# Scan layers of a four-layer sequence model: turning scan inputs by halves of 64 partitions, with a quarter of an earlier state's sum in the other half

## What is computed

```python
xs, z = jnp.split(h @ in_w, 2, axis=-1); xs = jax.nn.silu(xs)
proj = xs @ xproj_w
dt = jax.nn.softplus(proj[..., :D_INNER] + dt_bias)          # D_INNER = 512
Bm, Cm = proj[..., D_INNER:D_INNER + D_STATE], proj[..., D_INNER + D_STATE:]
A = -jnp.exp(A_log)
def step(hst, ins):
    dt_t, B_t, C_t, x_t = ins
    dA = jnp.exp(dt_t[:, :, None] * A)
    hst = hst * dA + (dt_t * x_t)[:, :, None] * B_t[:, None, :]
    y_t = jnp.einsum('bds,bs->bd', hst, C_t)
    return (hst, y_t)
...
y = jnp.swapaxes(ys, 0, 1) + xs * Dskip
return y * jax.nn.silu(z) @ out_w
```

## Time and profile before

| | us |
|---|---|
| median of 3 executions | 4431.58 (4429.39 to 4431.88) |
| the profiled execution | 4438.28, of which its span is 4436.4 |
| scans of layer 1, first to last | 294.3 to 1636.2 |
| scans of layer 3, first to last | 1945.5 to 4386.9 |
| TensorE busy / VectorE / ScalarE / GpSimd in the span | 4136.1 / 4006.7 / 3883.4 / 3654.9 |

### The profile page before, as it was taken

One profiled execution on the slowest core, in us unless ns is written; L12 is line 12 of the kernel. 1 busy time (PEld: TensorE's weight loads), 2 busy tenths in 40 slices (PEclk: granted clock), 3 DMA queues, 4 the chain that ended last, 5 costly groups with the idle time before them and its releaser, 6 DMA issues.

```text
span 4436.4 us, 109577 instructions
## 1 busy us (share of the span) xinstructions
PE 4136.1 (93%) x45534; PEld 3204.2 (72%) x45534; DVE 4006.7 (90%) x3859; ACT 3883.4 (88%) x6078; POOL 3654.9 (82%) x1360
## 2 busy tenths in 40 slices
PE   9999899899899988999999999999999999999998
PEld 6457677677677764458877777778777778777777
DVE  6669999899999986759999999999999999999996
ACT  4569899899999964569999999999999999999995
POOL 3338898889889973339999999999999899999995
PEclk8999999999999999999999999999999999999999
DMA  4012122121221221022232422422422422323221
GB/s 168 1 27 69 54 65 67 52 65 66 59 60 61 71 78 41 1 38 86 88 75 82 88 67 81 84 71 82 88 72 71 87 82 93 68 78 68 73 83 40
DMA packets 241499, 305.16 MB, mean 69 GB/s; under 512 B 116448, under 2 KB 175712, under 8 KB 241008
## 3 DMA queue, kind: packets, MB, share of 16 engines
q1 hardware_dynamic: 241008, 298.15, 23.8%
HBM read 289.84 MB, written 8.26 MB: 67 GB/s over the span
## 4 chain that ended last, share of the span: by engine, by line
ACT 40%; PE 36%; DVE 16%; issue 7%; POOL 1%; DVEq 0%; DMA 0%; SPq 0%; ACTq 0%; POOLq 0%
ACT weights_c L1814 10%; DVE work L2330 8%; PE psum L874 8%; ACT work L1831 8%; ACT work L1814 7%; PE psum L1166 7%; PE psum L1148 7%; PE psum L1145 5%; ACT weights_c L1831 5%; PE psum L1293 5%; DVE weights_c L2330 4%; ACT L1512 2%; ACT modulation L1814 2%; PE psum L1376 1%; PE psum L1086 1%
## 5 line engine op out<-in xcount | busy, mean ns | idle before, releaser
L2759 POOL TENSOR_TENSOR work<-work,weights_a 128x2048 f32<-128x2048 f32 x512 | 1976.8, 3870 | 119.7 <-DVE work L2330 93.7
L2330 DVE TENSOR_TENSOR_SCAN work<-weights_c,psum 128x512 f32<-128x512 f32 x1316 | 1509.2, 1204 | 89.7 <-PE psum L1148 77.5
L2759 POOL TENSOR_TENSOR weights_c<-weights_c,weights_a 128x2048 f32<-128x2048 f32 x256 | 989.7, 3872 | 39.6 <-DVE weights_c L2330 38.9
L1148 PE MATMUL psum<-ident,work 128*128 128x128 f32 x5464 | 935.9, 274 | 12.0 <-ACT work L1831 4.4
L1814 ACT ACTIVATE work<-work,decay 128x504 f32<-128x504 f32 x1172 | 822.7, 715 | 44.5 <-DVE weights_c L2330 24.8
L1148 PEld LDWEIGHTS psum<-ident,work 128*128 128x128 f32 x5464 | 666.0, 142 | 59.8 <-issue 33.0
L1148 PE MATMUL psum<-ident,weights_c 128*128 128x128 f32 x3752 | 695.9, 275 | 0.0
L2330 DVE TENSOR_TENSOR_SCAN work<-work,psum 128x512 f32<-128x512 f32 x586 | 675.3, 1202 | 19.8 <-PE psum L1148 15.0
L2330 DVE TENSOR_TENSOR_SCAN weights_c<-work,psum 128x512 f32<-128x512 f32 x586 | 675.7, 1202 | 15.8 <-PE psum L1148 15.3
L1166 PE MATMUL psum<-ident,work 64*128 64x64 f32 x16800 | 661.1, 229 | 8.7 <-POOL work L2759 7.6
L1166 PEld LDWEIGHTS psum<-ident,work 64*128 64x128 f32 x16800 | 588.7, 141 | 97.6 <-issue 72.9
(11 more groups left out here) (224 smaller groups left out, 6609.9 us busy)
## 6 DMA issues: line engine op xcount, KB each, us to landing
weights_a<-c_rows SPq DMA_DIRECT2D x384, 512.0 KB, 3.7
work<-b_diagonals SPq DMA_DIRECT2D x240, 128.0 KB, 2.2
weights_c<-b_diagonals SPq DMA_DIRECT2D x112, 128.0 KB, 2.1
b_diagonals<-weights_c SPq DMA_DIRECT2D x1, 4096.0 KB, 18.2
weights_c<-in_L_cond_fwd_in_w SPq DMA_DIRECT2D x8, 512.0 KB, 5.7
weights_c<-in_L_cond_fwd_xproj_w SPq DMA_DIRECT2D x4, 1024.0 KB, 7.1
weights_c<-in_L_cond_bwd_in_w SPq DMA_DIRECT2D x8, 512.0 KB, 5.5
weights_c<-in_L_cond_bwd_xproj_w SPq DMA_DIRECT2D x4, 1024.0 KB, 7.1
```

What stands on the lines that cost most here:

```text
L1148: last = nc.tensor.transpose(PS[:, bank, t * P:(t + 1) * P], buf["scaled"][s % INPUTS][t][:, j * P:(j + 1) * P], IDENT[:, :])
L2330: v.tensor_tensor_scan(buf["ring"][s % RING][:, along, j], buf["decay"][q % DECAYS[l]][:, along], PS[:, 4 + q % LOOKAHEAD, along], 0.0, AL ...
L2759: g.tensor_tensor(state, state, row.unsqueeze(2).broadcast_to([P, T, DC]), ALU.mult).then_inc(ss["prod_ready"], 1)
```

## The change

Each step now does a quarter of a sum along with its scan input. The scan input is done in two parts, partitions 0 to 63 of the tiles (turn 0) and 64 to 127 (turn 1), each a matmul of 64 partitions with 64 output columns. Behind each of the four comes one half transpose of the sum from the other 64 partitions (`add_half`), for one bank of the sum per step. Turn 1 waits until turn 0's last add has ended (`half_made`), since both turns write the same banks. The wait for a product of GpSimd now stands ahead of the scan input of the first of the four steps. The first and last state of each sum and run keep the block of 32. Pieces are no longer kept off any step.

```diff
     def piece(self, name, k):
-        step = self.start + int((self.at[name][0] + k * self.stride) * self.spread)
-        return step + 1 if step % DC == ADDED_AT else step
+        return self.start + int((self.at[name][0] + k * self.stride) * self.spread)
...
         for s in range(RUNS * states):
-            step = (s + 2) * DC + ADDED_AT + (1 if s % (states * together) == 0 else 0)
-            self.adds.setdefault(step, []).append(s)
+            opens, ends_run = s % (states * together) == 0, (s + 1) % states == 0
+            step = (s + 2) * DC + ADDED_AT + (1 if opens else 0)
+            for bank in (None,) if opens or ends_run else range(TT):
+                self.adds[step + (bank or 0)] = (s, bank)
...
+                    if q in adds_with and adds_with[q][1] == 0:
+                        products_made(adds_with[q][0])
...
+                    added, to = adds_with[q]
+                    begins, ends = opens_sums(added)
+                    half = P // 2
+                    for turn in range(2):
+                        if turn:
+                            pe.wait_ge(ss["half_made"], q_done[q])
+                        mine_rows = slice(turn * half, turn * half + half)
+                        for t in range(TT):
+                            out = PS[:, bank, t * P + turn * half:t * P + turn * half + half]
+                            if t < SCALED or fourth_by_pool(l, s):
+                                made_half = nc.tensor.matmul(
+                                    out, buf["scaled"][s % INPUTS][t][mine_rows, j * P:(j + 1) * P],
+                                    IDENT[mine_rows, mine_rows], start=True, stop=True, is_transpose=True,
+                                    tile_position=(turn * half, 0))
+                            else:
+                                made_half = nc.tensor.matmul(
+                                    out, buf["dtx"][r % 2][mine_rows, SCALED, j * P:(j + 1) * P],
+                                    buf["diagonal"][mine_rows, s // 2 % 2, s % 2, mine_rows], start=True, stop=True,
+                                    tile_position=(turn * half, 0))
+                            added_half = add_half(added, to, t, 1 - turn, begins and turn == 0 and t == 0,
+                                                  ends and turn == 1 and t == TT - 1)
+                        if turn == 0:
+                            added_half.then_inc(ss["half_made"], 1)
+                        else:
+                            made_half.then_inc(ss["input_ready"], 1)
+                    if to == TT - 1:
+                        added_half.then_inc(ss["sum_done"], 1)
...
+                def add_half(s, bank, k, g, start, stop):
+
+                    flat = buf["ring"][s % RING].rearrange("p t j -> p (t j)")
+                    rows, at = slice(g * P // 2, (g + 1) * P // 2), (bank * DC + k) * P
+                    return nc.tensor.matmul(PS[:, bank, k * P + g * P // 2:k * P + (g + 1) * P // 2],
+                                            flat[rows, at:at + P], IDENT[rows, rows], start=start, stop=stop,
+                                            is_transpose=True, skip_group_check=True, tile_position=(g * P // 2, 0))
...
+                adds_with = {q + LOOKAHEAD: a for q, a in pl.adds.items()
+                             if a[1] is not None and q + LOOKAHEAD < pl.scans}
...
-                    for s in pl.adds.get(q, ()):
-                        add_up(s)
+                    if q in pl.adds and q + LOOKAHEAD not in adds_with:
+                        add_up(*pl.adds[q])
...
-                        while at is not None and (at <= step and q not in pl.adds or step == pl.steps - 1):
+                        while at is not None and (at <= step or step == pl.steps - 1):
```

55 lines of the change are left out of this document (36 added, 19 removed).

## The result

| | before | after |
|---|---|---|
| median, us | 4431.73 (4429.39 to 4441.15, 4 executions) | 5278.5 (5209.74 to 5295.89, 4 executions) |
| ratio | | 1.181, interval 1.1766 to 1.1853 |
| profiled execution, its span | 4438.28, 4436.4 | 5295.89, 5293.9 |
| granted clock of TensorE, mean | 0.983 | 0.833 (0.830 to 0.850 in the four) |
| layer 1 / layer 3, first scan to last | 1341.9 / 2441.4 | 1703.5 / 2941.4 |

The change costs 847 us by the medians, against 386 forecast; the time lies far outside the range. In the profiled execution both scan layers pay, 361.6 and 500.0 us; the rest of the program keeps its length to within 5 us. All four executions have the low mean clock, so it belongs to the kernel.

What follows compares the result with a forecast made beforehand. VectorE's scans bound the scan layers; TensorE, with 461 us to spare, would gain 566 + 225 = 791 us of work and become the bound. With unused gaps that gave +386 on 4431.6, 4818 us; range 4620 to 4950.

Steps and rivals of the forecast that it cites:

- a falling clock: TensorE's granted clock falling from 0.98, listed last among the signs of a wrong forecast; nothing in it prices this.
- Pairs of halves: Scan-input and sum half transposes run together: a pair costs about 0.062 us, a full transpose 0.109.
- The half product: Fourth tile's product on halves: 0.109 us a pass, four passes a step; merged step 1.10 against 0.888, +566 us of TensorE.
- The wait: TensorE's half_made wait between a step's two parts: 0.283 us exposed, then 0.052 of load.
- The piece between halves: A piece between half-array steps takes 1.19 us instead of 0.86, +0.34 for crossings; 671 pieces, +225 us.
- What TensorE could use of its spare time: TensorE has 461 us to spare in layers 1 and 3; all but 26 and another 30 us usable.
- its first rival: Halved product costs 0.062 a pass: step 0.901, groups with a piece 3.89 against 3.47 us, +110, 4540 us; chance 0.09.
- What costs nothing: Earlier wait for GpSimd's product, sum_done, pieces one step earlier, other engines' work: no cost counted.
- VectorE's waits over 400 us: Sign of being right: VectorE's waits for scan inputs grow from 123 to over 400 us, first of all waits.
- Merged steps of 1.10: Sign of being right: merged steps take 1.10 us, and 0.78 in every third state of runs 2, 4 and 6.
- Runs 3 and 2 of layer 3: Sign of being right: run 3 of layer 3 is longer by 40 us, run 2 by 30.
- The faster one: Rival: even load outweighs crossings if the merged step is under 0.81 us; 4370 us, chance 0.04.

Runs made afterwards that it cites:

- the filled kernel: Changed kernel with four extra half transposes behind the half_made signal in each merged step, the wait kept: 4851.9 us, ratio 1.094.
- The cross experiment: Kernel before with one half transpose of the identity ahead of each product into bank 7: 4497.3 us, ratio 1.0142.
- The kernel with one wait in each whole scan input: Kernel before, with TensorE waiting for itself after the first transpose of each scan input: 4918.9 us, ratio 1.109.
- the pieces' steps: Kernel before with pieces allowed also at steps with an add block: 4454.7 us, ratio 1.0045.
- pairs of halves in each step: Changed kernel's sum spread as 4 pairs of half transposes a step, but behind a whole 128-partition scan input, with no exposed wait: 4786.0 us, one execution.
- the kernel with two waits: Kernel before, with TensorE waiting for itself after the first and the second transpose of each scan input: 5784.5 us, one execution.
- The two filled kernels: Changed kernel with four extra half transposes behind the signal, in every step 4851.9 us (ratio 1.094), in every second step 4885.3 us (1.102).
- the kernel without products: Changed kernel with the fourth tile of merged steps made by half transposes of the third tile's data, the wait kept: 4575.3 us, ratio 1.032.

## Why the prediction was wrong

**The sum priced all of TensorE's work at the full clock.** This is the step that failed by most. The forecast's last paragraph names a falling clock as something that nothing in it prices, gives it no rival and no chance, and ends the range at 4950. Three kernels cut the 847 us in two: without the wait 4414, with the wait filled 4852, with the wait open 5278. The wait itself is 438 us, at a clock that is not quite full (0.954 and 0.950 in the two kernels). Another 427 come from what the open gap lets happen to the clock. The shares hold for this order of taking away: the products alone, taken out with the wait left in, are worth 703 us, so they can't be added up over all causes. The traces agree on the size: scans of layer 1 at the low level come 1.94 us apart against 1.40 at the full level, 400 of them; in layer 3 it is 1.99 against 1.28, 407 of them. 400 x 0.54 + 407 x 0.71 = 505 us, and the same sum for the filled kernel is 102. The difference is 403 of the 427.

The filled kernel stands closest to what the forecast worked out, 4852 against 4818. That is luck: errors of opposite sign nearly cancel, as its terms show.

**Pairs of halves: right.** 0.062 was forecast for a pair. Steps without a product take 0.780 us against 0.779.

**The half product: pace right, reason wrong, and the merged step too long.** The passes come 0.11 to 0.12 us apart, as taken. But the load doesn't explain it: in the step shown above the load of the product's second pass (2702.30) is followed on the same 64 partitions by that of a half transpose after 0.05 us (2702.35). What sets the pace of the passes stays open. And the sum laid each part behind the end of the part before it. In fact the next step's first part runs on the free half while the second part's products pass, so the step is 0.94 us and not 1.10. The term is 2694 x (0.942 - 0.888) = +145 us instead of +566.

The rule that I weighed there (the Trainium skill, "TensorE: Matmul & The Clock Gate", LDWEIGHTS: load time by columns, not partitions) doesn't agree with the trace for transposes on 64 partitions: they come every 0.06 us, with the same 128 columns that take 0.11 on 128 partitions. Nor does it with the 0.05 behind the half product's load.

**The wait: right.** 0.283 was forecast; 0.281 is the step with it less the step without it (0.942 - 0.661), and 0.278 in the kernel before. The 0.052 of load behind it was counted too much: the product's second pass starts 0.35 us after the gated load (2703.29 against 2702.94), where the sum had 0.052 + 0.346 = 0.40.

**The piece between halves: too low.** +0.34 was forecast, with 0.38 as the bound. It is 1.35 - 0.86 = +0.49, and 1.20 - 0.86 = +0.34 in the kernel without the wait. The crossing was priced well; the rest is the overlap of two steps, 0.15 us, which a piece between them takes away. The cross experiment's 0.40 lies beside it. The term is 671 x 0.49 = +329 instead of +225.

**What TensorE could use of its spare time: far too much.** With these two terms TensorE gets 145 + 329 = 474 us more work, and 461 were to be spare. Used up but for 56 us, as the forecast had it, this would be 4500. The filled kernel is 418 us above the kernel before, about 100 of them at the low level. So about 300 of the 461 us could not be used. TensorE is only 3 steps ahead of VectorE, so the sum has to be made by groups that are no longer than that: where a piece comes every third step, 2 x 0.942 + 2.295 = 4.18 us stand against 3.47 of scans, and the steps between such groups, where TensorE would be early, cannot save anything for them. Layer 3 has 479 pieces, 413 of this kind and 66 of turns (1.82 a step, 3.70 a group): 413 x 4.18 + 66 x 3.70 + 611 x 1.126 (the median distance of scans) for the steps outside of groups = 2658 us, and 27 for the low level; the filled kernel takes 2677. The agreement is partly luck, for this is an estimate: of the distances between pieces there only 230 of some 480 are three steps, 129 are four and 63 two, and 66 pieces stand at steps without a product, where a group takes 3.54. The kernel with one wait in each whole scan input bears this out from the other side: its groups of 3.35 fit, and it could use 369 of the 461. The forecast made this very comparison in its first rival and not in its own sum. (Two small slips change nothing: 150 + 15 x 25 steps of 0.055 are 29 us and not 26, and a wait of 0.25 to 0.30 gives -97 to +50 over 2942 steps.)

**What costs nothing.** Of the points that the forecast put at nothing, one was tried alone, the pieces' steps: 20 us. The earlier wait for GpSimd's product was not tried by itself; without the self-wait all of it together is within the 4414.

**Signs named ahead.** VectorE's waits over 400 us (but third in the list, not first), the gap of near 0.28, 14,390 more instructions, 0.78 in steps with no product: as named. Merged steps of 1.10: not there. Runs 3 and 2 of layer 3 are longer by 58 and 69 us, for 40 and 30 named; in the filled kernel by 34 and 30. The falling clock: there.

**The rivals.** The one of a halved product at 0.062 a pass puts the step at 0.901, nearer to the 0.942 than the forecast's own 1.10, though its 0.06 holds for loads and not for passes. The faster one was right in its condition: a step under 0.81 wins; at 0.661 it does win, 0.4%.

**What stays open.** *Why this kernel's clock stays low and that of others does not.* Idle time alone isn't it: the two waits are half of each step of the kernel that has them, and its clock is 0.981. Halves with crossings aren't it: 0.990 with pairs of halves in each step. Half work in all of a step's scan input and sum but no wait gives 0.954, only in short falls. Nor is it enough that a step at the low level is longer than a scan, as the kernel with two waits shows. Halves in all of a step together with an open gap in each are there in the changed kernel and in the one without products, and these two have the lowest clocks. Taking away the gap, half of the gaps, the products or half the merged states each brought the clock up. But these two together don't force the low level either. The changed kernel's own trace has stretches of nothing but merged steps, with a product and without a piece, at both levels:

```profile
core 0: us, PE busy (x) PEld busy (x) DVE busy (x) ACT busy (x) POOL busy (x), PEclk, DMA share, GB/s
1930.00:1993.00 63.00, 59.15 (x1035) 50.99 (x1034) 62.21 (x56) 54.84 (x86) 56.02 (x18) 1.00 0.20 65
728.00:766.00 38.00, 36.33 (x459) 31.67 (x456) 30.79 (x32) 29.73 (x48) 25.40 (x9) 0.50 0.23 47
```

The first, at the end of layer 1, is at the full level for 63 us, the second at the low one for 38, with TensorE busy 94 and 96%. In the first the steps follow the scans, 1.107 us apart in the median; in the second they take 1.507 and hold the scans up. So the same instructions run at either level for long, and what takes the clock from one to the other isn't in them alone.

The Trainium skill ("TensorE: Matmul & The Clock Gate", What's actually happening) says that the gate goes by how busy TensorE has been. The two filled kernels agree with that in direction; the kernel with two waits, idle for longer and at 0.981, shows that idle time doesn't tell it alone, and the busy share of the profile doesn't either (94% here at 0.833, 93% there at 0.981). What the work on halves counts for was not measured apart. Nor is it settled why the kernel without products, whose steps have the larger share of gap, has a higher clock, 0.898. That its low steps of 1.187 nearly keep up with the scans may be a part of it.

*A version that wins* was not found. One would issue the first part of step `q + 1` between the parts of step `q`, so that the wait has work in front of it; it needs a further bank for scan inputs, and it wasn't tried.

## What to carry to other kernels

A wait of TensorE for its own last matmul cost 0.28 us each time here, unless other work was queued between the signal and the wait; so put something there, useful work if there is any. Price a change of TensorE's work by groups no longer than it may run ahead of its reader, not by the sum of spare time over a layer. And look at the granted clock by stretch as soon as a kernel has been changed to partial matmuls with gaps: work that is short enough at 2.4 GHz may be too long at 1.2, and then nothing catches up.

## What the runs showed of the hardware

- The clock can stay at the low level for 211.6 us while TensorE's rows are busy 96% of the time (2764 to 2966 us, another such stretch, has 194.9 of 202.0 us busy at 0.51). More matmuls, of no use and in no one's way, made the kernel 8% faster. Steps of the same instructions ran at the full level for 63 us and at the low one for 38.
- Work on the two halves of the partitions overlaps across steps, and not in program order: the next step's L1167 load at 2702.25 stands ahead of this step's second L1172 load at 2702.30.
- Transposes with loads of 64 partitions by 128 columns come 0.06 us apart, those of 128 by 128 0.11. The two passes of a product come 0.10 to 0.12 us apart on 32, 64 and 128 partitions alike (and 2702.18 to 2702.30).
- A half matmul between whole ones costs 0.40 us; one 128x512 product of two matmuls between halves costs 0.34 us, and 0.49 where two steps overlapped.
